# First stage of a two-stage attention and mixture kernel: slots of two units, blocks of 32 queries by 64 keys

## What is computed

```python
H, D, window_size = (16, 64, 32)
xn = rms_norm(x); qkv = xn @ w_qkv.T        # q, k, v: 16 heads of 64
q = apply_rope(q, cos, sin); k = apply_rope(k, cos, sin)
attn = jnp.einsum('bhqd,bhkd->bhqk', q, k) * scale
mask = (q_pos >= k_pos) & (q_pos - k_pos <= window_size)
attn = softmax(where(mask, attn, NEG))
out = jnp.einsum('bhqk,bhkd->bhqd', attn, v)
return out.reshape(B, T, H * D) @ w_out.T
```

## Time and profile before

| | |
|---|---|
| median of three runs | 1217.03 us (1214.63 to 1219.91) |
| the profiled execution | 1215.93 us; its span is 1213.9 us |
| PE busy | 1102.0 us (91%) |
| weight loads on PE | 901.6 us (74%) |
| DVE busy | 971.9 us (80%) |
| ACT busy | 921.6 us (76%) |
| POOL busy | 854.2 us (70%) |

### The profile page before, as it was taken

The page is one execution under the profiler, slowest core; times in us unless marked ns, Lnnn a source line. Parts: engine busy times, 40 slices in busy tenths (PEclk is TensorE's granted clock), DMA queues, the critical chain, the costliest instruction groups (busy, mean ns, idle before and its releaser), DMA issues. The chain is left out here.

```text
span 1213.9 us, 49597 instructions
## 1 busy us (share of the span) xinstructions
PE 1102.0 (91%) x17489; PEld 901.6 (74%) x17489; DVE 971.9 (80%) x4190; ACT 921.6 (76%) x3404; POOL 854.2 (70%) x685
## 2 busy tenths in 40 slices
PE   4899999999999999999999999947998985399994
PEld 2688888888888888888888887725777775388884
DVE  6898988898898888989988987645888764278885
ACT  2689989989899899899899897926777653166662
POOL 2787877877877777878778776645476767257777
PEclk9899999999999999999999999969898886599997
DMA  6776666766676767667667666534143212676300
GB/s 195 202 183 165 177 169 163 182 165 171 170 176 162 179 160 179 166 166 181 169 163 181 156 164 180 125 107 157 36 136 108 82 56 109 193 198 181 85 32 32
DMA packets 111026, 180.88 MB, mean 149 GB/s; under 512 B 19726, under 2 KB 64177, under 8 KB 110656
## 3 DMA queue, kind: packets, MB, share of 16 engines
q1 hardware_dynamic: 102944, 158.53, 50.6%
q0 software_dynamic: 6400, 16.82, 3.8%
q10 hardware_dynamic: 1440, 2.36, 0.7%
HBM read 35.20 MB, written 24.73 MB: 49 GB/s over the span
## 5 line engine op out<-in xcount | busy, mean ns | idle before, releaser
L612 POOL TENSOR_TENSOR qk<-mm,sw 128x1024 f32<-128x1024 f32 x128 | 305.1, 2383 | 102.4 <-DMA sw<-mm 102.2
L685 ACT ACTIVATE pr<-sm,mn 128x96 f32<-128x96 f32 x1024 | 368.5, 370 | 0.0
L618 POOL TENSOR_TENSOR pr<-pr,ri 128x768 f32<-128x768 f32 x128 | 189.1, 1478 | 67.1 <-DVE ri L540 66.9
L501 DVE TENSOR_TENSOR mm<-bank,cos 128x512 f32<-128x512 f32 x256 | 175.3, 685 | 70.1 <-PE bank L324 58.7
L685 ACT ACTIVATION_READ_ACCUMULATOR pr<-sm,mn 128x1 f32 x1024 | 202.0, 197 | 0.0
L513 DVE CUSTOM_DVE_ANT_0 sm<-bank,msk 128x96 f32<-128x96 f32 x1024 | 191.0, 251 | 3.9 <-PE bank L350 3.9
L502 DVE TENSOR_TENSOR mm<-bank,sin 128x512 f32<-128x512 f32 x256 | 173.9, 679 | 0.0
L377 PE MATMUL bank<-pT,vw 96*64 96x64 f32 x4096 | 148.3, 226 | 0.0
L377 PEld LDWEIGHTS bank<-pT,vw 96*64 96x64 f32 x4096 | 130.6, 138 | 17.2 <-issue 6.0
L676 ACT ACTIVATE pT<-bank 96x512 f32<-96x512 f32 x256 | 137.3, 588 | 0.0
L392 PE MATMUL bank<-ident,pr 128*96 128x128 f32 x1024 | 132.7, 273 | 0.0
(11 more groups left out here) (206 smaller groups left out, 2488.0 us busy)
## 6 DMA issues: line engine op xcount, KB each, us to landing
sw<-mm SPq DMA_DIRECT2D x512, 128.0 KB, 2.4
vw<-vn SPq DMA_DIRECT2D x128, 192.0 KB, 2.6
vw<-vn SPq DMA_DIRECT2D x128, 128.0 KB, 2.3
rr<-sorted_scratch SPq DMA_DIRECT2D x72, 192.5 KB, 2.7
vw<-vn SPq DMA_DIRECT2D x96, 64.0 KB, 2.2
xt<-in_x SPq DMA_DIRECT2D x16, 256.0 KB, 3.9
x_scratch<-x SPq DMA_DIRECT2D x16, 256.0 KB, 2.5
rr<-x_scratch SPq DMA_DIRECT2D x16, 256.0 KB, 3.0
```

Source lines behind the costliest of these rows:

```text
L501: dve.tensor_tensor(mm[s % 2][:, 0, j, :], PJ[u % 2][:, :], cos[:, :], ALU.mult)
L612: pool.tensor_tensor(qk[i % 2][:, :, 32:], mm[i % 2][:, 0, :, :], sw[i % 2][:, :, :], ALU.add)\
L618: pool.tensor_tensor(t, t, ri[i % 2][:, :].unsqueeze(2).to_broadcast([P, 8, WK]), ALU.mult)\
L685: ins = act.activation(pr[i % 2][:, h, p, :], ms_[i % 2][:, h, p, :], ACT.Exp, scale=-1.0, bias=mn[i % 2][:, h, p:p + 1], accum_out=sums[i ...
```

## The change

A slot now holds two units, 2p and 2p+1; there are 64 + 4 slots, and the lags are LS = 1, LT = 2, LO = 3, LW = 4, LY = 7 of them.

- Scores: blocks of 32 queries by 64 keys. 32 products for a unit (64 rows, 32 weight columns, 64 moving columns) in place of 16. Both units' scores stand back to back; each head's bank holds 256 columns of each unit. Masks, exponentials and the multiplication are over 64 columns in place of 96, as many operations as before.
- Turns: four transposes of 128x128 in place of eight of 128x96, into one bank (TR), and one copy of 128x512 in place of two of 96x512. The bank that is left goes to a second result bank (OB).
- v: the copy goes to vn, laid out for four parts; a second layout vs is shifted by 32 tokens with one or two DMAs a unit (96 and 32 partitions) in place of two or three.
- Value products: 32 for a unit (64 rows, 64 weight columns, 32 moving columns), both units back to back. The two copies out of the result are each over 128x512 for a head's half of both units, so still two copies for two units on each engine.
- The order of every engine's list is written anew, as the diff shows. PE: project, gather, values, gather, project, turn, values, turn, scores twice, value products twice. DVE: rope, inverse of the odd unit, rope, the low parts, both units' masks, inverse of the even unit, and then every fourth slot the statistics.
- Centring uses scalar_tensor_tensor in place of tensor_scalar.

The core of the diff:

```diff
-WK, NW = 96, T // 64
+WK = 64
+NP = NI // 2
-        PJ, SC, TR, OB, ACC = banks[0:2], banks[2:4], banks[4:6], banks[6], banks[7]
-        LS, LE, LT, LV, LO, LY = 2, 3, 4, 5, 6, 9
-        SLOTS = NI + LY
+        PJ, SC, TR, OB, ACC = banks[0:2], banks[2:4], banks[4], banks[5:7], banks[7]
+        LS, LT, LO, LW, LY = 1, 2, 3, 4, 7
+        SLOTS = NP + 4
+        def part(w):
+            g, j = divmod(w, 4)
+            return 2 * (g // 2) + j // 2, 2 * (g % 2) + j % 2
+                def shift(n):
+                    half, j = divmod(n, 4)
+                    v = vs[half % 2]
...
+                    sp.wait_ge(s_ve, n + 1)
+                    sp.dma_start(v[32:128, j, :], vn[half % 2][0:96, j, :]).then_inc(s_vd[half % 2], 16)
+                    if j < 3:
+                        sp.dma_start(v[0:32, j + 1, :], vn[half % 2][96:128, j, :]).then_inc(s_vd[half % 2], 16)
+                def turn(i):
+                    pe.wait_ge(s_nm, i + 1)
...
+                    for h in range(2):
+                        for m in range(2):
+                            ins = pe.transpose(TR[:, (2 * h + m) * P:(2 * h + m + 1) * P],
+                                               pr[i % 2][:, h, 2 * m:2 * m + 2, :].rearrange("p a k -> p (a k)"), ident[:, :])
+                def scores(i):
+                    e, t = i % 2, qk[i % 2]
+                    if i >= 2 and e == 0:
+                        pe.wait_ge(s_mx, 2 * i)
+                    pe.wait_ge(s_add, i + 1)
+                    for w in range(16):
+                        grp, c = part(w)
+                        for h in range(2):
+                            r = slice(64 * h, 64 * h + 64)
+                            o = 256 * e + 64 * grp
+                            ins = pe.matmul(SC[h][32 * c:32 * c + 32, o:o + 64], t[r, 0, 32 + 32 * w:64 + 32 * w],
+                                            t[r, 1, 32 * w:32 * w + 64], start=True, stop=True, skip_group_check=True)
+                    ins.then_inc(s_sc, 1)
+                def attend(p):
...
+                        for g in range(4):
+                            for jl in range(2):
+                                for h in range(2):
+                                    for jh in range(2):
...
+                                        ins = pe.matmul(OB[jh][64 * h:64 * h + 64, d:d + 32], v[r, g, k:k + 64],
+                                                        pT[e][r, o:o + 32], start=True, stop=True, skip_group_check=True)
```

PE's list:

```diff
+                for s in range(SLOTS):
+                    if s < NP:
+                        project(2 * s)
+                    if 0 <= s - LW < NP:
+                        gather(s - LW, 0)
+                    if s < NP:
+                        values(2 * s)
+                    if 0 <= s - LW < NP:
+                        gather(s - LW, 1)
+                    if s < NP:
+                        project(2 * s + 1)
+                    if 0 <= s - LT < NP:
+                        turn(2 * (s - LT))
+                    if s < NP:
+                        values(2 * s + 1)
+                    if 0 <= s - LT < NP:
+                        turn(2 * (s - LT) + 1)
...
+                    if 0 <= s - LS < NP:
+                        scores(2 * (s - LS))
+                        scores(2 * (s - LS) + 1)
+                    if 0 <= s - LT < NP:
+                        attend(s - LT)
```

VectorE's list:

```diff
+                def inverse(i):
+                    dve.wait_ge(s_exp, 2 * i + 2)
+                    if i >= 2:
+                        dve.wait_ge(s_nm, i - 1)
+                    dve.reciprocal(ri[i % 2][:, :], sums[i % 2][:, :]).then_inc(s_ri, 1)
+                for s in range(SLOTS):
+                    if s < NP:
+                        rope(2 * s)
+                    p = s - LT
+                    if 0 <= p < NP:
+                        inverse(2 * p + 1)
...
+                    if s < NP:
+                        rope(2 * s + 1)
...
+                    p = s - LS
+                    if 0 <= p < NP:
+                        masked(2 * p)
+                        masked(2 * p + 1)
+                        inverse(2 * p)
...
+                    if s % 4 == 2 and s // 4 + 2 < NB:
+                        layer_stats(s // 4 + 2)
```

ScalarE's list:

```diff
+                for s in range(SLOTS):
+                    if s < NP:
+                        keys(2 * s)
...
+                    if 0 <= p < NP:
+                        turned(2 * p)
+                    if s < NP:
+                        keys(2 * s + 1)
+                    if 0 <= p < NP:
+                        turned(2 * p + 1)
...
+                    p = s - LS
+                    if 0 <= p < NP:
+                        exponent(2 * p)
+                        exponent(2 * p + 1)
```

GpSimd's list:

```diff
+                for s in range(SLOTS):
+                    if 0 <= s - LT < NP:
+                        normalised(2 * (s - LT))
+                    if 0 <= s - LS < NP:
+                        rotated(2 * (s - LS) + 1)
+                    if 0 <= s - LT < NP:
+                        normalised(2 * (s - LT) + 1)
...
+                    if s < NP:
+                        rotated(2 * s)
```

More of the change, by code:

```diff
@@ L152, in program @@
         s_ve = sem("a_ve")
-        s_vd = [sem(f"a_vd{n}") for n in range(4)]
+        s_vd = [sem("a_vd0"), sem("a_vd1")]
         s_pv = sem("a_pv")
@@ new lines, in rope @@
+                def rope(i):
+                    for j in range(2):
+                        u = pj_use[("rope", i, j)]
+                        dve.wait_ge(s_pj, u + 1)
+                        if i == 0:
+                            dve.wait_ge(s_cs, 32)
+                        if i >= 2 and j == 0:
+                            dve.wait_ge(s_add, i - 1)
+                            dve.wait_ge(s_sw[i % 2], 64 * (i // 2))
+                        dve.tensor_tensor(mm[i % 2][:, 0, j, :], PJ[u % 2][:, :], cos[:, :], ALU.mult)
+                        dve.tensor_tensor(mm[i % 2][:, 1, j, :], PJ[u % 2][:, :], sin[:, :], ALU.mult).then_inc(s_rope, 1)
@@ L529, in _ @@
+                    if b is not None:
                         u = pj_use[("yt", b)]
@@ L625, in _ @@
                             next(sh)
-                        if r == 4:
+                            next(sh)
+                        if r == 1:
                             scale(b)
-                    i = s - LY
-                    if 0 <= i < NI and i % G == G - 1:
-                        b = i // G
+                        if r == 3 and b + 1 < NB:
+                            sh = shape(b + 1)
+                            next(sh)
+                    if s < NP:
+                        rotated(2 * s)
@@ new lines, in exponent @@
+                def exponent(i):
+                    for h in range(2):
+                        act.wait_ge(s_mx, 2 * i + h + 1)
+                        if i >= 2 and h == 0:
+                            act.wait_ge(s_tr, i - 1)
+                            act.wait_ge(s_ri, i - 1)
+                        for p in range(4):
+                            ins = act.activation(pr[i % 2][:, h, p, :], ms_[i % 2][:, h, p, :], ACT.Exp, scale=-1.0,
+                                                 bias=mn[i % 2][:, h, p:p + 1],
+                                                 accum_out=sums[i % 2][:, 4 * h + p:4 * h + p + 1])
+                        ins.then_inc(s_exp, 1)
```

424 lines of the change are left out of this document (182 added, 242 removed).

## The result

The kernel after takes 1414.49 us (median of four runs, 1403.41 to 1424.71), the kernel before 1215.83 (1213.97 to 1219.91) on the same chip. The ratio is 1.160, with an interval of 1.151 to 1.169. The forecast was 1242 us in a range of 1208 to 1276: the direction was right, the size was not.

A forecast was written before the change was run, and what follows sets the result against it. PE was taken to bound the kernel before at 5.90 us a unit; after, a ring of waits between engines. 1215.9 + 19 (ring with batch work) + 2 (fill and last slots) + 5 (clock) = 1242 us, range 1208 to 1276.

The forecast's parts named there:

- What bounds the kernel before: First stage: PE never waits and its own list sets the pace, 5.90 us a unit.
- What PE's work becomes: PE's work in a two-unit slot: 9.9 us against 11.50 before, a gain of 1.6 if PE still set the pace.
- the second stage that I left as untouched: The prediction listed the second stage among the other parts, priced at nothing.
- Scores 0.58 a unit: Score products on PE, 64 records a unit: 0.58 us, bounds 0.44 and 0.90, against 0.64 before.
- Value products (0.93) and turns: On PE: value products stay at 0.93 us a unit; eight turns a slot at 0.11 take 0.87, saving as much.
- The floor for every record's start: Rival, PE's scores: 0.021 us may be the least distance between records; 1.5 us a slot, +98 us, 1340; chance 0.01.
- The ring: Waits from masks through exponentials, inverse, rope, values and scores to the next masks set the pace: 11.45 us a slot, +19 us.
- The clock: PE's clock falls after half of 15 idle times of 2.1 us in slots with the statistics: +5 us, bounds 0 and +25.
- the fourth rival: PE's waits keep its clock at 1.2 GHz for long stretches: 1290 us or more, chance 0.04; sign: falls every second slot.
- The sum: Whole kernel: 1215.9 + 19 + 2 + 5 = 1242 us, 2% slower.
- the forecast had +2: The fill and the last slots are longer by a slot's lag: +2 us.
- the three slower ones: Scores on only four tiles, 1283 us (0.12); clock long at 1.2 GHz, 1290 or more (0.04); record start floor, 1340 (0.01).

The follow-up runs named there:

- e_wide_fill: Kernel after with half as many small products, twice as wide, plus five large products per slot giving back the saved PE time; 1272.32 us, ratio 1.042 to the kernel before.
- e_dense: Kernel before with each score product issued eight times into the same place; 2228.55 us, ratio 1.831.
- e_spread: Kernel after with the same PE instructions reordered: value products a slot later, each small group between large products; 1365.76 us, ratio 1.122 to the kernel before.
- e_inv: Kernel after with only the even unit's reciprocal moved on DVE from behind the masks to behind the next slot's first rope; 1542.90 us, ratio 1.266 to the kernel before.
- v_unit: The change's small blocks in the one-unit slots, lags and order of the kernel before; ratio 1.005 to the kernel before.
- e_dense2: Kernel before with 112 score products of 32 columns added per unit, in four-tile order, ahead of its own scores; 2029.77 us, ratio 1.613.

## Why the prediction was wrong

- *What bounds the kernel before*: right. PE, to the last 0.1 us a unit.
- *What PE's work becomes*: **the step that failed.** It priced each product by the distance of records in rows where they follow closely, and left it at 64 for 32 records a unit. That PE's list would have 576 entries in a slot for some 330, 512 of them within 3.5 us, had no term, because in the first stage before no row shows delivery as a limit. `e_wide_fill` puts the delivery of these entries, with the clock that it costs, at 142 us of the 199. The trace before did have the sign, in the second stage that I left as untouched, in the very kind of product from whose rate I argued. From the trace of before, PE's order of time:

```profile
846.04 1.02 PE L1047 MATMUL bank<-fk,fq 32*32 32x32 f32 x96
849.07 0.36 PE L1047 MATMUL bank<-fk,fq 32*32 32x32 f32 x32 [2.00 <-issue]
```

  96 products, 2 us of nothing, 32 products. And a group of the earlier trace rows that I quoted for its 105 ns carried "5.8 <-issue".
- *Scores 0.58 a unit*: mis-sized. From scores to value products it is 1.53 us in a slot (508.20 to 509.73), 1.43 without the switch, 0.72 a unit: inside my bounds of 0.44 and 0.90. That is 0.27 a slot, 17 us. Value products (0.93) and turns were right to 0.02.
- *The floor for every record's start*, 0.01, on which the trace decided: score records are 11 ns apart (1.60 less 0.22, over 127). It was rightly low. It named the right risk, that number counts, in the wrong place: not per record but per 256 entries.
- *The ring*: its parts are there. DVE waits 57.9 us in 53 times, 1.09 each, for the last exponential (1.2 forecast), and exponentials take 334 ns (0.34). With delivery taken out, the slot is 12.77; the ring's 12.1 with 0.27 for the scores gives 12.4, so 0.4 stay unexplained. But it did not set the pace after: PE's wait for rope was swallowed by the stops (17.3 us in all from 100 to 900 us).
- *The clock*, +5 with a bound of 25: PE's busy time per slot grew by 1.3 us at equal work, some 84 us, in part beside other waits. I had bound it by idle times that the ring makes; the stops make more of them. The sign that I gave for the fourth rival is there: a low stretch begins in 39 of the 64 slots. But the waits for rope that it blamed are not the source: `e_wide_fill`, with more of them and no stop, has 11 low stretches in place of 49.
- *The sum*: 26 us forecast, 17 of scores and 142 of delivery make 185, and 199 were measured; 14 are left. By the profile some 6 of them lie behind the start of the last slot, where the forecast had +2 and 8 are seen; the rest I can't place.
- *The rivals*: the three slower ones, at 1283, 1290 and more, and 1340 us, had 0.17 together and lay above the range's upper end of 1276, so "about 0.1" on that side did not fit my own chances. Even the farthest was 74 us short. None was about a resource that the trace of the first stage had not yet shown at its limit.

The Trainium skill (Runtime: NRT & Kernel Launch, Instruction fetch mechanics) says that instructions are refilled in blocks of 256 while the current one is executed, and that the cost of crossing a boundary is "mostly hidden". The trace agrees on the 256. On the cost it agrees in `e_dense`, where a block lasts at least 4.1 us, and in `e_spread`, and disagrees in the kernel after where it lasts 1.4 to 3 us: 2 us a boundary.

## What to carry to other kernels

Count the instructions per microsecond on PE, not only their durations: smaller blocks double the entries. In the kernel after every block of 256 entries that passed in under 3 us was followed by a stop; in `e_dense`, where none passed in under 4.1, there was none. Spread such loops between large products, or use fewer and wider ones; here 330 entries a slot in place of 576 were worth 142 us at equal PE work. An idle time that says "issue" inside a loop without waits is a row to price, wherever in the trace it stands; that it falls at a constant position modulo 256 is what tells delivery from a wait that the profile misses, as VectorE's in `e_inv`. Before an operation is moved on one engine, read what is queued behind its reader on the next.

## What the runs showed of the hardware

- Blocks of 256 PE entries: where PE stopped, it went on 2.9 to 4.8 us after the boundary before (seven stops of the kernel after, 505 to 590 us), with 1.25 to 1.5 of it behind the packet's landing. The packet's start varied: 0.0 to 0.35 us after the boundary for most in `e_dense`, 1.4 us in the median of the kernel after's stops and up to 6.9. There the swap transfers filled the queues (94% beside the packet). That these delay it was not tested.
- A late packet can stop PE behind a slow block too: 13 of the 19 stops of `v_unit` follow blocks of 4.5 to 5.4 us, and in the median of the 19 the packet starts 3.25 us after the boundary ahead.
- The stops over 0.7 us inside a loop of the first stage lie at one position, 193 modulo 256 counting all of PE's records, its sequencer's too, in all eight kernels that have any.
- Score records of 64x96 are 21 ns apart in the kernel before, where four tiles alternate, and 34 in `e_dense`, where two do and write the same place eight times; records of 64x32 with four tiles 14 ns (`e_dense2`), of 64x64 in the scores after 11 ns.
- Behind a stop of 1.9 us the granted clock fell to 0.50 until about 502 us, through a second stop; behind one of 2.1 us it stayed at 1.00.
